# VectorE's side work cut into smaller parts at other places in the step, and expert weights loaded one expert at a time (gated cross-attention and a top-2 mixture of 8 experts)

## What is computed

```python
Q, K, V = split_heads(query @ Wq + bq), split_heads(key @ Wk + bk), split_heads(value @ Wv + bv)
attn = softmax(einsum('bhqd,bhkd->bhqk', Q, K) / sqrt(16))
xattn = (attn @ V) @ Wo + bo
x = x + tanh(g_xattn[0]) * xattn(layernorm(x), ctx, ctx)
scores = softmax(xf @ w_router.T)               # xf: the second layernorm of x, 3584 tokens
expert_weights, expert_indices = top_k(scores, 2)
y = einsum('eth,ehd->etd', silu(xf @ w1[e]) * (xf @ w3[e]), w2)     # 8 experts, 352 hidden
x = x + tanh(g_ffn[0]) * sum over the two chosen experts of weight * y
```

## Time and profile before

| | |
|---|---|
| median of 3 runs | 883.62 us (882.75 to 885.35) |
| the profiled execution | 888.39 us, its span 886.7 us |
| PE / PEld busy | 841.7 us (95%) / 684.6 us (77%) |
| DVE / ACT / POOL busy | 491.4 / 413.7 / 476.3 us |
| longest chain | PE 85%, DVE 5%, DMA 3%, issue 3%, ACT 2% |
| first stage, second stage | to about 602 us, from there to the end |

### The profile page before, as it was taken

How to read it: one execution, slowest core, us unless ns; L and a number is a source line. 1 busy time by engine, 2 the same in 40 slices (tenths; PEclk the granted TensorE clock), 3 DMA queues, 4 the chain that set the end, 5 groups by cost and what they waited for, 6 DMA issues and landing times.

```text
span 886.7 us, 21416 instructions
## 1 busy us (share of the span) xinstructions
PE 841.7 (95%) x7209; PEld 684.6 (77%) x7209; DVE 491.4 (55%) x1163; ACT 413.7 (47%) x1086; POOL 476.3 (54%) x570
## 2 busy tenths in 40 slices
PE   7899999999999999999999999879999999999995
PEld 6678888788877878878888888767777777777773
DVE  4566767766675776776778677653442222222221
ACT  3256556555655556655665566454423222222221
POOL 7345343445545545555546646353677765666552
PEclk9899999989999999999999999999999999999998
DMA  6957677667667557657665665464344443434432
GB/s 179 205 139 193 150 174 172 174 159 167 169 159 176 150 137 169 157 117 173 144 152 128 145 151 122 97 181 106 57 63 64 63 70 55 72 61 66 64 57 30
DMA packets 99426, 112.29 MB, mean 127 GB/s; under 512 B 28860, under 2 KB 80708, under 8 KB 99320
## 3 DMA queue, kind: packets, MB, share of 16 engines
q1 hardware_dynamic: 79304, 92.48, 43.8%
q0 software_dynamic: 18512, 17.60, 12.6%
q10 hardware_dynamic: 1504, 0.85, 0.5%
HBM read 35.48 MB, written 17.53 MB: 60 GB/s over the span
## 4 chain that ended last, share of the span: by engine, by line
PE 85%; DVE 5%; DMA 3%; issue 3%; ACT 2%; ACTq 0%; POOL 0%; POOLq 0%; DVEq 0%
PE ps L1400 17%; PE ps L1151 9%; PE ps L1461 9%; PE ps L1145 9%; PE ps L1128 9%; PE ps L1113 9%; PE ps L1156 8%; PE ps L1256 3%; DMA stack<-negmax_t 3%; DVE negmax L854 3%; PE ps L1419 2%; PE ps L1315 2%; PE ps L1344 2%; PE ps L1248 1%; PE ps L1230 1%
## 5 line engine op out<-in xcount | busy, mean ns | idle before, releaser
L854 DVE TENSOR_REDUCE negmax<-ps 112x2 f32<-112x750 f32 x256 | 239.8, 938 | 144.4 <-PE ps L1145 138.0
L586 ACT ACTIVATE probs<-ps 125x448 f32<-125x448 f32 x384 | 209.6, 547 | 157.7 <-PE ps L1113 141.6
L389 POOL DMA_DIRECT2D stack<-negmax_t x128 | 68.2, 536 | 248.8 <-PE ps L1113 124.2
L1113 PE MATMUL ps<-stack 97*125 97x224 f32 x768 | 191.8, 333 | 5.7 <-DMA stack<-negmax_t 4.2
L1113 PEld LDWEIGHTS ps<-stack 97*125 97x125 f32 x768 | 130.2, 192 | 33.9 <-DMA stack<-negmax_t 4.6
L1145 PE MATMUL ps<-stack 96*112 96x376 f32 x512 | 139.9, 355 | 12.4 <-DVE negmax L854 12.3
L505 POOL DMA_INDIRECT out_dram<-y,idx x63 | 100.6, 1597 | 72.2 <-issue 36.0
L1067 DVE TENSOR_TENSOR h<-silu,ps 128x352 f32<-128x352 f32 x63 | 32.8, 521 | 147.9 <-PE ps L1400 132.5
L687 ACT ACTIVATE silu<-ps 128x352 f32<-128x352 f32 x63 | 29.3, 465 | 182.2 <-PE ps L1400 172.7
L1151 PE MATMUL ps<-wv_sb,ctx_t 128*125 128x256 f32 x384 | 106.7, 402 | 7.3 <-ACT xn_t L633 6.8
L1461 PE MATMUL ps<-w_sb,h_t 128*128 x378 | 92.3, 380 | 0.7 <-ACT h_t L693 0.7
(11 more groups left out here) (221 smaller groups left out, 1223.5 us busy)
## 6 DMA issues: line engine op xcount, KB each, us to landing
stack<-split SPq DMA_DIRECT2D x252, 150.0 KB
ctx_t<-in_ctx_dram SPq DMA_DIRECT2D x32, 375.0 KB, 3.9
stack<-split SPq DMA_DIRECT2D x127, 94.0 KB
stack<-split SPq DMA_DIRECT2D x127, 56.0 KB
out_dram<-xa SPq DMA_DIRECT2D x32, 112.0 KB, 3.4
xn_scratch<-xn SPq DMA_DIRECT2D x32, 112.0 KB, 3.2
xa<-in_x_dram SPq DMA_DIRECT2D x7, 448.0 KB
w_sb<-in_L_ffn_w_dram SPq DMA_DIRECT2D x8, 352.0 KB
```

Of the source, the lines that this page charges most:

```text
L389: gp.dma_start(dst[:, :, SKP + SQ * h:SKP + SQ * h + SQ], negmax_t[4 * h:4 * h + 4, half, :].bitcast(f32)).then_inc(s_nmrow[half][c % NSLO ...
L586: act.activation(probs[:, n % NP, :], ps[0:KW, EXPB + k % 2, 0:4 * SQ], ACT.Exp).then_inc(s_exp, 1)
L854: dve.tensor_reduce(negmax[:, half, :, p4], ps[0:SQ, m1:m2 + 1, 0:SK], axis=AX.X, op=ALU.max, negate=True).then_inc(s_max, 1)
L1113: last = pe.matmul(ps[0:KW, EXPB + k % 2, QW * m:QW * m + QW], stack[:, place_of(b), p, KW * ch:KW * ch + KW], stack[:, place_of(b), p, SK ...
```

## The change

**VectorE.** `route` part 1 is cut in two (the second half is part 6, at k = 8 of i % 4 = 2), part 4 as well (first half at k = 5 of i % 4 = 3, second half as part 7 at k = 8). Part 5 moves from k = 2 to k = 5 of i % 4 = 0. The statistics are taken by `rows_of`: one sequence each at k = 5 and k = 8 of i % 4 = 1, and the other two, with `halve1`, at k = 1 of i % 4 = 0; `polish1` moves from k = 1 to k = 8 of that step. The 12 pieces of the early map get places of their own in steps 24 to 29.

**ScalarE.** The copy to `xn2_t` stands ahead of the exponentials of k = 10 instead of behind them; `root1` moves from k = 0 to k = 4, the routing's exponential from k = 5 to k = 3.

**SyncE.** Each DMA brings one expert's block (176 KB, for w2 128 KB or 96 KB): two a step in steps 3 to 7, one a step in steps 8 to 21. The copies within DRAM go two a step in steps 1 to 6. `w3_hi` and w2 are sent by `last_weights` in 32 DMAs, the first 16 in step 30, the others in step 31, each waiting for one exponential group of TensorE more; their wait for the last negated maxima is gone. TensorE's program is the same but for the counts that it waits for.

```diff
--- before.py
+++ after.py
-        MAP_STEPS = [GB * SNAP + n for n in (8, 9, 12, 13)]
+        MAP_AT = [(GB * SNAP + n, k) for n, k in ((8, 2), (9, 1), (9, 2), (9, 5), (9, 8), (10, 2), (11, 2), (12, 1), (12, 2), (12, 8), (13, 1), (13, 2))]
...
-            def load_w2(c):
-                n = min(P, F - P * c)
-                sp.dma_start(w2_sb[0:n, c, :, :], w2[:, P * c:P * c + n, :].rearrange("e p d -> p e d")).then_inc(s_w2, 16)
+            def last_weights(first, end):
+                for n in range(first, end):
+                    sp.wait_ge(s_exp_ps, 12 * (B - 2) + 2 * n // 3 + 1)
+                    e, c = n % NE, n // NE - 1
+                    if c < 0:
+                        sp.dma_start(w3_hi[:, e, :], w3[e, P:2 * P, :]).then_inc(s_w13, 16)
+                    else:
+                        m = min(P, F - P * c)
+                        sp.dma_start(w2_sb[0:m, c, e, :], w2[e, P * c:P * c + m, :]).then_inc(s_w2, 16)
...
-                if i == LAST - 1:
-                    sp.wait_ge(s_exp_ps, 12 * (B - 2))
-                    sp.sem_inc(s_met_sp, 1)
-                    sp.wait_ge(s_stack[(B - 1) % NSLOT], stacked(B - 1))
-                    sp.wait_ge(s_nmrow[0][(B - 1) % NSLOT], 32 * ((B - 1) // NSLOT + 1))
-                    sp.dma_start(w3_hi[:, :, :], w3[:, P:2 * P, :].rearrange("e p f -> p e f")).then_inc(s_w13, 16)
-                    load_w2(0)
...
-                if 1 <= i <= B - GB * (SNAP + 1):
-                    n = GB * (SNAP + 1) + i - 1
+                for n in range(GB * (SNAP + 1) + 2 * i - 2, GB * (SNAP + 1) + 2 * i) if 1 <= i <= (B - GB * (SNAP + 1)) // 2 else ():
...
-                if 3 <= i < 15:
-                    e2 = (i - 3) % 4 * 2
-                    src, dst, k = ((w1, w1_sb[:, 0], 0), (w1, w1_sb[:, 1], 1), (w3, w3_lo, 0))[(i - 3) // 4]
-                    sp.dma_start(dst[:, e2:e2 + 2, :], src[e2:e2 + 2, P * k:P * k + P, :].rearrange("e p f -> p e f")).then_inc(s_w13, 16)
+                for n in (2 * i - 6, 2 * i - 5) if 3 <= i < 8 else (i + 2,) if 8 <= i < 22 else ():
+                    src, dst, h = ((w1, w1_sb[:, 0], 0), (w1, w1_sb[:, 1], 1), (w3, w3_lo, 0))[n // NE]
+                    sp.dma_start(dst[:, n % NE, :], src[n % NE, P * h:P * h + P, :]).then_inc(s_w13, 16)
...
+                if i == LAST - 2:
+                    sp.wait_ge(s_stack[(B - 1) % NSLOT], stacked(B - 1))
+                    last_weights(0, 2 * NE)
                 if i == LAST - 1:
-                    sp.wait_ge(s_nmrow[1][(B - 1) % NSLOT], 32 * ((B - 1) // NSLOT + 1))
-                    for c in range(1, FC):
-                        load_w2(c)
+                    last_weights(2 * NE, (FC + 1) * NE)
...
+                    if k == 10 and r is not None:
+                        act.wait_ge(s_xn2_ps, r + 1)
+                        wait(act, s_lg_ps, r - GB + 1)
+                        act.activation(xn2_t[:, r % GB, :, :], ps[:, BC, 0:DC * SQ], ACT.Copy).then_inc(s_xn2_t, 1)
...
-                    if k == 0 and i % GB == 0 and 1 <= i // GB + 1 < NG:
+                    if k == 4 and i % GB == 0 and 1 <= i // GB + 1 < NG:
...
-                    if k == 10 and r is not None:
-                        act.wait_ge(s_xn2_ps, r + 1)
-                        wait(act, s_lg_ps, r - GB + 1)
-                        act.activation(xn2_t[:, r % GB, :, :], ps[:, BC, 0:DC * SQ], ACT.Copy).then_inc(s_xn2_t, 1)
-                    if k == 5 and settled_in(i) is not None:
+                    if k == 3 and settled_in(i) is not None:
...
+            def rows_of(g, rows):
+                dve.wait_ge(s_x[g % 4], 16 * (g // 4 + 1))
+                for n in rows:
+                    last = dve.bn_stats(st1[:, n, :], xrow(GB * g + n))
+                link(last)
+                for n in rows:
+                    last = dve.bn_aggr(mv1[:, g % 2, n, :], st1[:, n, :])
+                if GB - 1 in rows:
+                    link(last)
+                    halve1(g)
...
-                    if k == 1 and i % GB == 0 and 1 <= i // GB + 1 < NG:
+                    if k == 8 and i % GB == 0 and 1 <= i // GB + 1 < NG:
                         polish1(i // GB + 1)
-                    if k == (11 if i == -1 else 8) and (i % GB in (1, 3) or i == -2):
-                        g, first = (1, 0) if i == -2 else ((i + 7) // GB, 0) if i % GB == 1 else ((i + 5) // GB, 2)
-                        if (1 if first or i == -2 else 2) <= g < NG:
-                            dve.wait_ge(s_x[g % 4], 16 * (g // 4 + 1))
-                            for n in (first, first + 1):
-                                last = dve.bn_stats(st1[:, n, :], xrow(GB * g + n))
-                            link(last)
-                            for n in (first, first + 1):
-                                last = dve.bn_aggr(mv1[:, g % 2, n, :], st1[:, n, :])
-                            if first:
-                                link(last)
-                                halve1(g)
+                    if i == -2 and k == 8:
+                        rows_of(1, (0, 1))
+                    if i == -1 and k == 11:
+                        rows_of(1, (2, 3))
+                    if i >= 0 and i % GB == 1 and (i + 7) // GB < NG and k in (5, 8):
+                        rows_of((i + 7) // GB, (k // 8,))
+                    if i > 0 and i % GB == 0 and i // GB + 1 < NG and k == 1:
+                        rows_of(i // GB + 1, (2, 3))
...
-                    if i in MAP_STEPS and k in (1, 5, 8):
-                        early_map(3 * MAP_STEPS.index(i) + (1, 5, 8).index(k))
+                    if (i, k) in MAP_AT:
+                        early_map(MAP_AT.index((i, k)))
...
+                    if routed is not None and k == (5 if i == B - 1 else 8):
+                        route(routed, 6)
...
-                    if settled is not None and k == 7:
+                    if settled is not None and k == 5:
                         route(settled, 4)
-                    if settled_in(i - 1) is not None and k == 2:
+                    if settled is not None and k == 8:
+                        route(settled, 7)
+                    if settled_in(i - 1) is not None and k == 5:
...
-                        pe.wait_ge(s_w13, 208)
+                        pe.wait_ge(s_w13, 16 * 4 * NE)
...
-                        pe.wait_ge(s_w2, 16 * FC)
+                        pe.wait_ge(s_w2, 16 * FC * NE)
```

More of the change, by code:

```diff
@@ L760, in route @@
                     link(dve.tensor_tensor(eq, eq, over_b(first_e[:, :]), ALU.mult))
+                if part == 6:
                     link(dve.tensor_reduce(col, eq, axis=AX.X, op=ALU.max))
@@ L786, in route @@
                     link(dve.reciprocal(inv, inv))
+                if part == 7:
                     gate = pay[:, first:first + n, :, 1].bitcast(f32)
@@ L1069, in _ @@
                     route(NU - 2, 4)
+                    route(NU - 2, 7)
                     heads_out(B - 1)
@@ L1087, in _ @@
                     route(NU - 1, 1)
+                    route(NU - 1, 6)
                     route(NU - 1, 2)
@@ L1091, in _ @@
                     route(NU - 1, 4)
+                    route(NU - 1, 7)
                     route(NU - 1, 5)
```

## The result

The changed kernel took 868.76 us in the median of four runs (865.57 to 873.62), the kernel before beside it 883.7 us: a ratio of 0.9835, with a 95% interval of 0.980 to 0.987. The forecast was 868.0. A second measurement gave 873.72 us and 0.9877 (0.985 to 0.990). The number was right. The experiments show that it was right for partly wrong reasons.

What follows compares the result with a forecast made beforehand. TensorE, busy 841.7 of 886.7 us, bounds the kernel; only idle time and clock can be won. Terms -10.1 - 4.0 + 0.9 - 4.0 + 0.6 = -16.6 us from 888.4 give 871.8, adjusted to the runs' median: 868 us, range 860 to 876.

Steps and rivals of the forecast that it cites:

- VectorE's waits, -10.1: Steps 7, 11, 15, 19: TensorE's waits for VectorE's reduces of the maxima go, clock included, -10.1 us.
- the lock for `half` at k = 1: i % 4 = 0, k = 1: shared ports make `half` cost about 1.10 us, not 0.17; place just full.
- ScalarE's copy, -4.0: k = 10, steps 3 to 28: TensorE's 0.31 us wait on the copy goes, 0.2 won per step, -4.0 us.
- The late rows, +0.9: Steps 8, 12, ... 28: rows of negated maxima leave 2.3 us late, net +0.9 us, bounds 0 and +9.4 without clock.
- the four x-load steps: Steps 8, 12, 16, 20: x load lies in the queue, late rows cost 0.7 us a step, 2.8 us in all.
- in a step without an x load that is enough: Late rows leave 3.4 us before TensorE needs them; median landing takes 2.6 us, so no wait there.
- The spell of 1.7: Late-row steps: one spell of TensorE's lower clock, priced at 1.7 us from step 12.
- a rival of +3 to +6: Side work waits at its new places, k = 1 overflowing, or the copy gives nothing: 871 to 874 us, chance 12%.
- The last weights, -4.0: Steps 30 and 31: smaller last weight pieces avoid the late last row and lower clock, -4.0 us, bounds 0 and -5.2.
- 290 GB/s, below the 366, so no backlog builds: End of SyncE's queue: 176 KB pieces every 0.6 us stay below the DMAs' 366 GB/s.
- the last row to be in time but for 0.2: Step 31: last row of negated maxima, 2.4 us waited for before, would be only 0.2 us late.
- the end doesn't gain: Rival: small pieces slow both last rows, the clock falls as before: 872 us, or 875 if both wait; chance 15%.

Runs made afterwards that it cites:

- Run 12: Kernel after, slots at k=2, masks at k=5, last weights' first 16 pieces in pairs behind index loads, others after last row landed: 864.88 us, 0.9769.
- run 9: Kernel after with ScalarE's copy at k=10 again behind the exponentials: 885.09 us, ratio 1.0000.
- run 5: The changed kernel itself, unchanged, timed on another chip: 873.72 us, ratio 0.9877.

## Why the prediction was right, and where it wasn't

The result hits the forecast by 0.8 us, and the sum doesn't deserve it: errors of both signs cancelled, and that they did is luck.

**VectorE's waits, -10.1.** Right as a step: 9.9 us left steps 7, 11, 15 and 19 with VectorE's pieces alone. The trace of the kernel after gives 11.1 there, 1.2 of it the copy's. The size rests on one execution, though: these four steps lost 10.1 us to ordinary ones in the trace of before, 12.2 with the copy alone and 8.6 with SyncE's queue alone, since the clock fell in two, two and one of them. What I drew from the lock for `half` at k = 1, that it would take 1.1 us beside GpSimd's normalization, didn't come: 0.17 us in all six steps, though GpSimd's 1.22 us had begun 0.7 us before it. The place held anyway.

**ScalarE's copy, -4.0.** The mechanism was right and the term too small: -7.3 us. I set its bounds to 0.17 and 0.31 us, from VectorE's idle time and the wait's own length. It was 0.29 in ordinary steps, inside the bounds but near the upper one, where I took 0.2; and 0.57 in the steps with rank products, outside them and where I took less.

**The late rows, +0.9.** (By its own terms, 2.8 + 1.7 against 3.7, this is 0.8.) I had the 2.3 us of lateness (2.9 measured in step 8) and the four x-load steps, where I took 0.7 each, 2.8 in all; they cost 0.73, 0.27, 0.34 and 1.18, 2.5 in all. What failed is "in a step without an x load that is enough": step 24 waited 1.35, and 1.0 to 2.1 in all seven traces with the slots at k = 5. The spell of 1.7 that I priced in didn't come in this execution. The cost depends on what else is in the rings: with pairs of weights before them, the same rows cost 1.7 to 2.4 us in steps 8 and 12, with a lower clock. With the slots and the masks back, 10.8 us are won in one comparison on the same chip and 7.6 in the other, so two pieces that the change moved cost about as much as all of VectorE's part was to bring.

**Masks at k = 8.** I named this risk only for `half`, and priced side work at new places as a rival of +3 to +6. It came at a place that I hadn't looked at: part 6 at k = 8, in step 22, where GpSimd's queries run. 1.86 us. The Trainium skill, "SBUF — State Buffer", section "SBUF: two separate sides", has the lock between the two engines extend to VectorE's instructions with two SBUF inputs, beside a GpSimd instruction that reads SBUF. Step 22 agrees (1.76 and 1.16 us), and so do the other five steps, more mildly: 0.38 to 0.47 against 0.19.

**The last weights, -4.0.** Wrong: -0.3 us, not to be told from nothing (0.9888 against 0.9877). The failing step is "290 GB/s, below the 366, so no backlog builds", and with it "the last row to be in time but for 0.2". SyncE issues faster than I took it to, and the DMA engines were busy for 0.97 of the first block. That block made the row of half 0 late, which was in time before. The row of half 1 stayed late, by 1.3 to 2.7 us in 11 of the 14 traces. Run 12 shows 5.4 us from its issue to its landing with no weights issued in that time, so what holds it stays open. The rival "the end doesn't gain" came true in mechanism: both last rows late, the clock at 0.66 from 575 to 585 us. Its 872 would have been the forecast with the other terms as they stood.

**The sum.** By the parts measured alone it would be -5.4 us; the whole is -11 to -15. So the parts are worth more together than alone, but which needs which is shown only in part. The pair of the copy with SyncE's queue wasn't run, so what VectorE's pieces add to the two others isn't known; on top of either alone they add nothing that can be told from zero. On top of VectorE's pieces and the copy, SyncE's queue brings 5.2 us on the same chip (5.7 against 10.9). For this there is a mechanism in the traces: in steps 8 and 12, three kernels with pairs of early weights waited 1.7 to 2.4 us for rows (VectorE's new order in all), and the granted clock of all six windows was below 1.00; four kernels with single pieces waited 0.3 to 1.2, with the clock at 1.00 in all eight. The two groups differ by 5 to 6 us in these two steps. The timed runs point that way in one comparison, with overlapping intervals (0.9935 without the new queue, 0.9888 with its early pieces), and not in the other (0.9846 with pairs, 0.9877 with single ones). How much is the early pieces' stays open. Open as well is why the copy earns more on top of the other two (-11 to -15 us) than alone (-7.3): the step lengths show 8 us of it. Part of the rest may be clock, whose median in the timed executions is 0.981 in run 9 and 0.984 in run 5, while the copy alone didn't raise it (0.979 against 0.980 before).

## What to carry to other kernels

A piece of side work moved out of one engine's wait has to be followed to who waits for it: here the slots, 2.9 us later, held GpSimd's queue and with it rows that TensorE needs. Two pieces moved back, these slots and the masks, won 8 to 11 us, about as much as the relief itself. Price a short stall that recurs by the distance between the instructions around it, not by the wait that the profile lists, and measure the parts of a change in pairs too, since alone two of these three showed nothing. Before a large transfer is split to thin it out, compare the rate at which the queue issues the pieces with what the DMAs can move. Here the two were about the same, and the block of small pieces kept the DMA engines about as busy as the large ones had (0.97 against 1.08).
